# A quantized FFN behind cross attention: gate and up weights kept as bare FP4 codes, scaled per group at the PSUM banks

## The reference, cut to what matters

```python
def _dequant_fp4(packed_i32, scales_f16, group_size):       # groups of 128 inputs
    nib = w[:, :, None] >> shifts & jnp.uint32(15)
    vals = _FP4_LUT[nib.astype(jnp.int32)].reshape(out_f, in_p * 8)
    s_full = jnp.repeat(scales_f16.astype(jnp.float32).T, group_size, axis=1)
    return vals * s_full
def _L0_ffn_ref(x, gate_up_packed, gate_up_scales, down_packed, down_scales):
    gate_up = jnp.einsum('bsh,oh->bso', x, w_gu)             # 512 -> 2 x 1408
    gate, up = (gate_up[..., :I], gate_up[..., I:])
    h = jax.nn.silu(gate) * up
    y = jnp.einsum('bsi,hi->bsh', h, w_down)                 # 1408 -> 512
    rms = jnp.sqrt(jnp.mean(y * y, axis=-1, keepdims=True) + EPS)
    return y / rms
x = x + jnp.tanh(g_ffn[0]) * _L0_ffn_ref(_layernorm(x, axis=-1), ...)
```

## Time and profile before

| | |
|---|---|
| median of 3 runs | 724.83 us (723.75 to 725.41) |
| the profiled execution, its own time | 725.4 us |
| its span, first to last instruction | 723.5 us |
| mean granted TensorE clock | 0.935 |
| busy: TensorE, weight loads | 636.1 us (88%), 574.9 us (79%) |
| busy: VectorE, ScalarE, GpSimd | 374.2 us (52%), 224.6 us (31%), 110.9 us (15%) |
| start of the first gate and up matmul | 405.99 us |
| end of the last decoded piece's products | 451.4 us |

### The profile page before, as it was taken

How to read it: one execution, slowest core, us unless ns; L and a number is a source line. 1 busy time by engine, 2 the same in 40 slices (tenths; PEclk the granted TensorE clock), 3 DMA queues, 4 the chain that set the end, 5 groups by cost and what they waited for, 6 DMA issues and landing times.

```text
span 723.5 us, 12567 instructions
## 1 busy us (share of the span) xinstructions
PE 636.1 (88%) x4594; PEld 574.9 (79%) x4594; DVE 374.2 (52%) x836; ACT 224.6 (31%) x645; POOL 110.9 (15%) x132
## 2 busy tenths in 40 slices
PE   1699979999789989899546877999999999999997
PEld 1598869888788868788434767899989989989994
DVE  6745535565455654567995899422422242242221
ACT  2754445334453453433210011212202212221210
POOL 5710120002100030000000011212201211221220
PEclk9988979999799998999856998999999999999999
DMA  8330020110201100021120311220022001011001
GB/s 274 134 96 3 1 92 1 35 58 0 91 0 45 45 0 0 0 73 60 31 63 5 110 66 42 67 94 1 1 60 66 1 29 65 0 29 58 0 0 44
DMA packets 20178, 33.34 MB, mean 46 GB/s; under 512 B 2988, under 2 KB 6700, under 8 KB 20140
## 3 DMA queue, kind: packets, MB, share of 16 engines
q1 hardware_dynamic: 20140, 32.85, 14.5%
HBM read 26.29 MB, written 6.55 MB: 45 GB/s over the span
## 4 chain that ended last, share of the span: by engine, by line
PE 65%; DVE 19%; ACT 6%; issue 6%; POOL 1%; DMA 1%; SPq 1%; ACTq 0%; DVEq 0%; POOLq 0%
PE bank L258 43%; PE bank L1458 13%; PE bank L1310 3%; ACT probs L678 3%; DVE nmax L886 2%; PE bank L1286 2%; DVE wgu_lo L1023 2%; DVE pT_lo L891 2%; DVE vb_lo L854 2%; ACT vb_hi L658 1%; PE bank L1297 1%; DVE fp L1018 1%; DVE wgu_hi L1021 1%; DVE fp L1014 1%; PE bank L1343 1%
## 5 line engine op out<-in xcount | busy, mean ns | idle before, releaser
L258 PE MATMUL bank<-mT_hi,wgu_hi 128*128 128x320 f32 x440 | 138.6, 315 | 10.2 <-DVE hidden L1173 8.9
L258 PE MATMUL bank<-mT_lo,wgu_hi 128*128 128x320 f32 x440 | 137.9, 313 | 0.0
L258 PE MATMUL bank<-mT_hi,wgu_lo 128*128 128x320 f32 x440 | 137.8, 313 | 0.0
L678 ACT ACTIVATE probs<-bank,nmax 100x96 f32<-100x96 f32 x256 | 66.1, 342 | 132.4 <-DVE nmax L886 132.4
L258 PEld LDWEIGHTS bank<-mT_hi,wgu_hi 128*128 128x128 f32 x440 | 84.3, 192 | 11.9 <-issue 10.3
L258 PEld LDWEIGHTS bank<-mT_lo,wgu_hi 128*128 128x128 f32 x440 | 84.5, 192 | 0.2
L1170 DVE SCALAR_TENSOR_TENSOR hidden<-tgate,bank 128x320 f32<-128x320 f32 x55 | 26.8, 487 | 111.8 <-ACT tgate L799 111.8
L258 PEld LDWEIGHTS bank<-mT_hi,wgu_lo 128*128 128x128 f32 x440 | 84.3, 192 | 0.0
L606 POOL TENSOR_TENSOR hT_lo<-hidden,hT_hi 128x320 fp32r<-128x320 f32 x55 | 49.9, 908 | 189.6 <-ACT hT_hi L803 189.6
L799 ACT ACTIVATE tgate<-bank 128x320 f32<-128x320 f32 x55 | 24.0, 437 | 168.0 <-PE bank L258 139.9
L1458 PE MATMUL bank<-wdn_hi,hT_hi 128*128 128x512 f32 (+1 forms) x143 | 56.2, 393 | 0.0
(11 more groups left out here) (129 smaller groups left out, 1415.4 us busy)
## 6 DMA issues: line engine op xcount, KB each, us to landing
xn<-in_x SPq DMA_DIRECT2D x16, 200.0 KB
xa<-in_x SPq DMA_DIRECT2D x16, 200.0 KB
x_scratch<-gate SPq DMA_DIRECT2D x16, 200.0 KB
ctx_raw<-in_ctx_tail SPq DMA_DIRECT2D x4, 768.0 KB, 6.9
xb<-x_scratch SPq DMA_DIRECT2D x5, 512.0 KB, 3.9
fp<-x_scratch SPq DMA_DIRECT2D x10, 256.0 KB, 2.7
out_x<-words SPq DMA_DIRECT2D x10, 256.0 KB, 2.1
words<-in_dn_packed SPq DMA_DIRECT2D x6, 256.0 KB
```

Source lines behind the costliest of these rows:

```text
L258: last = nc.tensor.matmul(out_ap, lhs(a, t), rhs(b, t), start=t == 0 and p == 0, stop=t == tiles - 1 and p == 2)
L678: last = nc.scalar.activation(probs[i % 2][:, cols], SC[i % HPG][0:L, cols], ACT.Exp, bias=nmax[:, i % 4, b:b + 1])
```

## The change

What it does, in parts.

1. The gate and up weights are the codes alone, which fp32r holds exactly. So there is one weight tile per FF tile and two passes (times mT high, times mT low): 16 matmuls instead of 24. decode of such a piece has no scale any more; its last stage is a copy from fp16 to fp32r. Its codes come in one transfer, laid out so that one k tile holds one scale group.
2. Each of the 4 scale groups has a bank of its own: products fills 8 banks a unit (4 gate, 4 up) out of a ring of six, banks 0 to 5 (slot_bank, open_slot). ScalarE scales the banks of groups 0 and 1 into two part tiles, with one scale per partition (scale_product). VectorE adds the scaled banks of groups 2 and 3 onto them (scale_add). GpSimd adds the two part tiles (gate_sum, up_sum). tanh reads the sum; gated and times_up, both with two SBUF tiles, take the place of L1170 and L1173. The tokens are normalised in four pieces of 128 columns instead of one of 512.
3. down runs in chunks of 3 matmuls beside gate and up of the next group: 2 or 3 output tiles a group, so 2 or 3 chunks a unit. The hidden tiles lie in a ring of 640 tokens. The loops over groups are written out instead of looped in hardware. mT is doubled, so that the next group's tokens are transposed at t = 5, 6, 7.
4. The schedule of decoding: 15 pieces in steps 6 to 15 of attention's last cycle (11 gate and up, 4 down), two pieces each in steps 9 to 12 and 15; the last two pieces at t = 2 and 4 of group 0. ScalarE waits for the last store of x1 (s_stored) before group 0, not after it. All three transpositions of group 0 come ahead of the output projections.

The diff, cut to its core:

```diff
-        wgu = [[sb(phase_b, f"wgu{t}_{half}", [128, KT, 256], F32R) for half in ("hi", "lo")] for t in range(FT)]
+        wgu = [sb(phase_b, f"wgu{t}", [128, KT, 256], F32R) for t in range(FT)]
...
+        ROUND = (2, 3, 4, 5, 0, 1)
+        TURN_AT = (5, 6, 7)
+        SLOTS = [("turned", 0, m) for m in range(3)]
+        for jj in range(FGROUPS):
+            for tt in range(FT):
+                SLOTS += [("turned", jj + 1, m) for m in range(3) if TURN_AT[m] == tt and jj + 1 < FGROUPS]
+                SLOTS += [("product", FT * jj + tt, p) for p in range(2 * KT)]
+        SLOT_AT = {slot: q for q, slot in enumerate(SLOTS)}
...
-        EARLY_AT = {i: i - 7 for i in range(7, STEPS)}
-        EARLY = len(EARLY_AT)
+        EARLY_AT = {6: (0,), 7: (1,), 8: (2,), 9: (3, 4), 10: (5, 6), 11: (7, 8), 12: (9, 10), 13: (11,), 14: (12,), 15: (13, 14)}
+        EARLY = sum(len(pieces) for pieces in EARLY_AT.values())
+        LATE_AT = {2 * i + 2: EARLY + i for i in range(PIECES - EARLY)}
...
+                if n >= FT + 2:
+                    sp.wait_ge(s_scaleb, n - FT - 1)
                 if n < FT:
-                    cols = slice(256 * n, 256 * n + 256)
-                    for half in range(2):
-                        p = slice(64 * half, 64 * half + 64)
-                        sp.dma_start(words[s][p, 0:256], gu_packed[:, cols]).then_inc(s_words[s], 16)
-                        sp.dma_start(scale[s][p, 0:256], gu_scales[:, cols].unsqueeze(1).broadcast_to([4, 16, 256]))\
-                          .then_inc(s_words[s], 16)
+                    sp.dma_start(words[s][:, :], gu_packed[n].unsqueeze(0).broadcast_to([4, 32, D])).then_inc(s_words[s], 16)
...
+            def gate_sum(j, t):
+                n = FT * j + t
+                a, b = part[n % 2][0]
+                pool.wait_ge(s_ed, 4 * n + 2)
+                nc.gpsimd.tensor_tensor(a[:, :], a[:, :], b[:, :], ALU.add).then_inc(s_gate_sum, 1)
...
+            for j in range(FGROUPS):
+                for t in range(FT):
+                    for n in tiles_done(j, t):
+                        rms_tile(n)
+                    gate_sum(j, t)
+                    if t == 2 and j + 1 < FGROUPS:
+                        ffn_rstd(j + 1)
+                    if t:
+                        hidden_lo(j, t - 1)
+                    elif j:
+                        hidden_lo(j - 1, FT - 1)
+                    up_sum(j, t)
...
+            def scale_product(j, t, i, k):
                 n = FT * j + t
+                if n >= 2:
+                    act.wait_ge(s_h, n - 1)
+                act.wait_ge(s_gu, 2 * KT * n + KT * i + k + 1)
+                nc.scalar.activation(part[n % 2][i][k][:, :], product_bank(j, t, i, k)[:, 0:TG], ACT.Copy,
+                                     scale=scale32[:, t, i, k:k + 1]).then_inc(s_ea, 1)
...
+            act.wait_ge(s_unit, 1)
+            act.wait_ge(s_stored, 1)
+            for j in range(FGROUPS):
                 for t in range(FT):
+                    for n in tiles_done(j, t):
+                        square(n)
+                    for k in range(2):
+                        scale_product(j, t, 0, k)
+                    if t:
+                        hidden_hi(j, t - 1)
+                    elif j:
+                        hidden_hi(j - 1, FT - 1)
+                    if t in TURN_AT and j + 1 < FGROUPS:
+                        mT_hi(j + 1, TURN_AT.index(t))
+                    for k in range(2):
+                        scale_product(j, t, 1, k)
+                    tanh_gate(j, t)
...
+                    dve.wait_ge(s_dec, n + 1)
+                    nc.vector.tensor_copy(wgu[n][:, :, :].rearrange("p k c -> p (k c)"), code.bitcast(F16)).then_inc(s_whi, 1)
...
+                for g in range(KT):
+                    cols = slice(128 * g, 128 * g + 128)
+                    last = nc.vector.tensor_scalar(mn[m][0:rows, cols].rearrange("t (e p) -> t p e", e=4),
+                                                   xb[0:rows, m, cols].rearrange("t (p e) -> t p e", e=4), mv[0:rows, m, 0:1],
+                                                   rstd[0:rows, m:m + 1], ALU.subtract, ALU.mult)
+                last.then_inc(s_mn, 1)
...
+            def scale_add(j, t, i, k):
                 n = FT * j + t
+                onto = part[n % 2][i][k - 2][:, :]
+                dve.wait_ge(s_gu, 2 * KT * n + KT * i + k + 1)
+                dve.wait_ge(s_ea, 4 * n + 2 * i + k - 1)
+                nc.vector.scalar_tensor_tensor(onto, product_bank(j, t, i, k)[:, 0:TG], scale32[:, t, i, k:k + 1], onto,
+                                               ALU.mult, ALU.add).then_inc(s_ed, 1)
...
+            def gated(j, t):
+                n = FT * j + t
                 dve.wait_ge(s_tg, n + 1)
+                if n >= 2:
                     dve.wait_ge(s_hlo, n - 1)
+                nc.vector.scalar_tensor_tensor(hidden[n % 2][:, :], tgate[n % 2][:, :], 1.0, part[n % 2][0][0][:, :], ALU.add, ALU.mult)\
                   .then_inc(s_sg, 1)
+            def times_up(j, t):
+                n = FT * j + t
                 dve.wait_ge(s_sg, n + 1)
+                dve.wait_ge(s_up_sum, n + 1)
+                nc.vector.tensor_tensor(hidden[n % 2][:, :], hidden[n % 2][:, :], part[n % 2][1][0][:, :], ALU.mult).then_inc(s_h, 1)
...
+            for j in range(FGROUPS):
+                for t in range(FT):
+                    for n in tiles_done(j, t):
+                        mean_square(n)
+                    if t:
+                        times_up(j, t - 1)
+                    elif j:
+                        times_up(j - 1, FT - 1)
+                    for k in (2, 3):
+                        scale_add(j, t, 0, k)
+                    if t in TURN_AT and j + 1 < FGROUPS:
+                        mT_lo(j + 1, TURN_AT.index(t))
+                    if j + 1 < FGROUPS:
+                        if t < 3:
+                            ffn_stats(j + 1, t)
+                        elif t < 6:
+                            ffn_normalise(j + 1, t - 3)
+                    for k in (2, 3):
+                        scale_add(j, t, 1, k)
+                    gated(j, t)
+                    for n in tiles_done(j, t):
+                        output_tile(n)
+                    if j == 0 and t in LATE_AT:
+                        decode_all(LATE_AT[t])
...
+            def open_slot(*slot):
+                q = SLOT_AT[slot] - len(ROUND)
+                if q < 0:
+                    return
+                kind, at, p = SLOTS[q]
+                if kind == "turned":
+                    pe.wait_ge(s_mtlo, 3 * at + p + 1)
+                elif p % KT < 2:
+                    pe.wait_ge(s_ea, 4 * at + 2 * (p // KT) + p % KT + 1)
+                else:
+                    pe.wait_ge(s_ed, 4 * at + 2 * (p // KT) + p % KT - 1)
...
+                for k in range(KT):
+                    open_slot("product", FT * j + t, KT * i + k)
+                    for half in (HI, LO):
+                        last = nc.tensor.matmul(product_bank(j, t, i, k)[:, 0:TG], wgu[t][:, k, 128 * i:128 * i + 128], mT[j % 2][half][:, k, :],
+                                                start=half == HI, stop=half == LO)
+                    last.then_inc(s_gu, 1)
...
+                pe.wait_ge(s_hlo, FT * ((128 * n + rows - 1) // TG) + c + 1)
+                for p, (a, b) in enumerate(PASSES):
+                    last = nc.tensor.matmul(bank[6 + slot][0:rows, :], hT[a][:, c, cols], wdn[c // 2][b][:, c % 2, :],
+                                            start=c == 0 and p == 0, stop=c == FT - 1 and p == 2)
+                last.then_inc(s_dn, 1)
...
+                    chunks = chunks_beside(j, t)
+                    products(j, t, 0)
+                    for n, c in chunks[:1]:
+                        down(n, c)
+                    products(j, t, 1)
+                    for n, c in chunks[1:]:
```

More of the change, by code:

```diff
@@ L450, in _ @@
                 phase_barrier(sp)
-                for n in range(EARLY + 2):
+                for n in range(PIECES):
                     load_piece(n)
@@ L627, in _ @@
+            for n in tiles_done(FGROUPS, 0):
+                rms_tile(n)
+            hidden_lo(FGROUPS - 1, FT - 1)
+            for n in TILES_BESIDE[FGROUPS]:
+                rms_tile(n)
         @block.scalar
@@ L831, in _ @@
-            for i in range(3):
-                square(PAIRS, i, True)
+                    for n in tiles_done(j, t):
[8 more added lines that the diff above has]
+                        mT_hi(j + 1, TURN_AT.index(t))
@@ L1131, in _ @@
                     decode_all(n)
-                ffn_stats(0)
+                for m in range(3):
+                    ffn_stats(0, m)
                 for m in range(3):
@@ L1215, in _ @@
-            for i in range(3):
-                output_tile(PAIRS, i, True)
+            for j in range(FGROUPS):
[22 more added lines that the diff above has]
+                        decode_all(LATE_AT[t])
@@ L1218, in _ @@
```

(29 more changed lines are left out.)

409 lines of the change are left out of this document (168 added, 241 removed).

## The result

The changed kernel takes 762.91 us (median of 4 runs, 761.19 to 764.61) against 724.29 for the one before in the same comparison: ratio 1.0532, 95% interval 1.0503 to 1.0562. Slower, as forecast, but by 5.3% where the forecast was 2.4%. The profiled span is 761.4 us; the prediction's was 740.4.

What follows compares the result with a forecast made beforehand. Bound before: TensorE in four of five groups; after: the serial VectorE-GpSimd loop. Attention to 421.9, 55 units 254.6, exceptions 3.4, 21.6, 2.4, 8, 2.5, tail 25, clock 1: span 740.4, time 742 us, range 702 to 764.

Steps and rivals of the forecast that it cites:

- how late the codes come: Attention's last cycle: waits for codes of 1 us in step 6, 2.2 in steps 9 to 12, more at down pieces.
- The end of attention: Attention's last cycle, with 15 pieces decoded for 9: 13.3 us more, bounds 5 and 20; first FFN unit starts at 421.9.
- What TensorE gives up: FFN: 440 of 1320 gate and up matmuls go, 64.5 us; a unit then needs TensorE 3.72 or 4.40 us beside down chunks.
- The ordinary unit: FFN, one tile of one group: serial loop through VectorE and GpSimd, 4.24 us plus 0.39 of port contention, 4.63 us.
- t=2: FFN units at this tile: ffn_rstd waits in GpSimd's queue ahead of hidden_lo and up_sum, 0.84 us more, 4 times, 3.4 us.
- The cut normalisation: FFN units at t=3 to 5: four pieces and GpSimd wait for each other, 1.8 us more in 12 units, 21.6 us.
- A: Rival, FFN units at t=3 to 5: the normalisation in four pieces does not block GpSimd, 21.6 us less, 720; chance 0.22.
- Late decoding: Group 0 of the FFN: pieces 15 and 16 decoded behind gated, on the path, 8 us.
- B: Rival, FFN: no port is ever contended on the path, units under 4.5 us in the median, 699 us; chance 0.13.
- C: Rival, FFN: TensorE at half clock in a quarter of 44 units, 31 us more, 773 us; chance 0.10.
- D: Rival, FFN: other engines keep under 3.7 us a unit, so the change gives what TensorE gives up, 658 us; chance 0.05.
- main case: Whole kernel: the forecast of 742 us with its own range of 727 to 757; chance 0.50.

Runs made afterwards that it cites:

- the kernel with repeated rows: The changed kernel with codes already repeated in DRAM, so each load of words is one plain 128-row transfer: 737.53 us, ratio 1.0189.
- the interleaved: The changed kernel with copies innermost in loads (32 rows outermost), down scales in two loads, normalisation as one plain tensor_scalar: 721.53 us, ratio 0.9964.
- split ones: The changed kernel with each load of words issued as four loads of 32 rows (eight of 16 for the last piece): 748.37 us, ratio 1.0326.
- the kernel that left the chain where it was: The interleaved kernel with three up products added on VectorE and GpSimd's up_sum gone: 711.88 us, ratio 0.9828.

## Why the prediction was right in direction and wrong in size

**The step that failed: how late the codes come.** "its load is issued at 324.89 and lands some 2.7 us later", "0.9 us in three of them, 2.2 in all", for the down pieces "some 2.4 us late" and "1.2 of waiting for the second". Together 6.8 us of waiting; 38.1 were measured, 31.3 more: 4.7 for 1 in step 6, 20.6 for 2.2 in steps 9 to 12, 12.8 for 3.6 at the down pieces. The FFN starts 30.5 us late: the 31.3, 3.5 more of waiting for the last residual (4.2, and 0.7 before), which no term held, and some 4 less in the other terms together. The end of attention, forecast at 13.3 us more with bounds of 5 and 20, came to 43.8. The mechanism (a second-next load has one step to come, and each down piece stands behind a wait) was right, its price was not. The 2.7 us was taken from the row of fp<-x_scratch, also 256 KB, a load of 128 plain rows. The load that the change adds has a dimension of 4 copies outermost. From the first issue of a pair to the first instruction behind the wait it takes 8.2 us (352.76 to 360.94), because the transfer runs at 94 to 101 GB/s with a quarter of the DMA engines' time in use (0.25, 0.26); at 128 plain rows the share is 0.98 and the rate 348. That the form alone does it, and not bytes or issues, is shown by the kernel with repeated rows; that 32 rows outermost are enough, by the interleaved and the split ones. The diff showed the form, and the kernel before has loads of that form too: its down pieces, whose landing the prediction didn't price apart. One is issued at 408.72, and the trace of before shows its rate, at a quarter of the engines' time (columns as in the earlier trace rows):

```profile
411.00:412.00 1.00, 1.00 (x9) 1.00 (x8) 0.96 (x4) 0.00 (x0) 0.00 (x0) 1.00 0.27 100
```

The Trainium skill (DMA: Bandwidth & Descriptors, Rules for kernel authors) says that a leading broadcast dimension of c copies confines the whole DMA to at most c engines. The trace agrees: 4 copies, a quarter of the share. It was the rule to weigh here, and the prediction weighed others.

**What TensorE gives up, and the bound passing to the other engines: right in groups 1 and 3.** TensorE is busy 43.6 of 54 us from 506 to 560, for the most part group 1, and from its first gate and up matmul to its last the kernel takes 287.8 us (444.4 to 732.2), against 289.6 before (406.0 to 695.6), with a third fewer of them. In group 4 it is not so: with 3 down chunks a unit TensorE needs the forecast's own 4.40 us, and it is busy 65.26 of the 66 us up to 735. There the bound stays with TensorE, or the two can't be told apart, and the mark "TensorE idle in each unit" did not come.

**The ordinary unit: 4.40, forecast 4.63.** In groups 1 and 3, where TensorE needs 3.72, the serial links came as worked out (4.24). The contention was there and smaller: gated 0.65 for 0.48, up_sum 1.13 for 0.88, of which 0.16 reaches the unit, not 0.39. 55 times 0.23 is 12.7 us less. The experiments correct the reading: the port weighs more than the row of the unit shows, as the order decides which instruction meets which. Taking hidden_lo off the chain made it dearer, taking up_sum away altogether gained 0.53 a unit.

**The exceptions.** t=2: 1.27 a unit, forecast 0.84. The cut normalisation: 1.3, forecast 1.8; A had at most 0.1 here. The order came as drawn, the second piece waiting for gate_sum and the third for hidden_lo, so A falls; each wait costs 0.58 us and not 0.88. The plain one, with the same elements, is 1.1 cheaper. Late decoding: 6.9 us (3.9 and 3.0), forecast 8. First x1: 2.7, forecast 2.5. mT_lo at t=5: 0.3 beside the cut normalisation, forecast 0.6. Not foreseen: at t=6 and 7, 1.7 to 3.5 us a group, 9.6 in all; TensorE waits there for mT_lo to free its bank (18.5 us of waiting in all), but that this wait is the cause was not tested. Without the first x1 the extras sum to 39.3 us for 35.4.

**The other rivals.** B, no contention: its mark, a median unit under 4.5 us, was met (4.40 for an ordinary unit, 4.49 as the median of all), which is 12.7 of its 21 us, but gated and up_sum are stretched in that unit and the cut normalisation cost its price, so the case as a whole did not come. C, the clock: granted 0.97 to 1.00 in groups 1 to 4 (0.73 in the window of group 0); the 1 us for it was not needed. D, the change gives what TensorE gives up: not as it stands; 658 us was reached by no kernel here, the best is 710.

**The sum.** Attention's end +30.5, the FFN -9.0, the tail +0.5, the clock -1: 21.0 us, from 740.4 to 761.4. The time lies within the range, but above the main case's own 757; the range reached that far for the clock, which had no part in it. That the range holds the time is luck.

What stays open: the kernel before was not run with plain-row loads for its down pieces, so what it would gain is not known; whether the units at t = 6 and 7 are long for the turned tile's bank; and which of two bounds, TensorE or the chain through GpSimd, holds the units of groups 2 and 4.

## What to carry to other kernels

Price a load by its form, not by its bytes: look for a dimension of copies outermost, in the diff and in the windows' DMA share, and put the rows outermost and the copies inside, if need be by another order of the contraction; here that, with the plain normalisation that the new order allows, took the changed kernel from 5% slower to level. When a chain runs through two engines that share a port, reordering moves the collisions; doing away with an instruction on the fuller engine, even for one more on the other, removes them. And where a chain is moved one tile later, look at every buffer that its last instruction reads: here, with two sets of partial tiles, the wait came back at their writer, and a third set took 28.7 us off, though no further than the kernel that left the chain where it was (711.9 us; the intervals overlap).
